# A fused alignment and FFN kernel: dense lead products on TensorE, and clears and mask preparation moved from GpSimd to VectorE ahead of the context's landing

## What is computed

```python
def align_one(small, large):                 # small: context 64x256, large: layernorm(x) 512x256
    D = sqrt(maximum(|small|^2 + |large|^2 - 2 small @ large.T, 0))
    R = dtw_cost(D)        # R[i,j] = D[i,j] + min(R[i-1,j], R[i,j-1], R[i-1,j-1])
    i_idx, j_idx, valid = backtrack(R)       # argmin of diagonal, up, left
    return zeros(512, 256).at[j_idx].add(small[i_idx] * valid)

x = x + vmap(align_one)(ctx, layernorm(x))
x = x + quantised_linear(relu(fixed_quant(quantised_linear(layernorm(x), w1, b1))), w2, b2)
```

## Time and profile before

| | us |
|---|---|
| median of 3 runs | 184.52 |
| the three runs | 184.53, 183.70, 184.52 |
| span of the profiled execution, first to last instruction | 182.2 |
| around the span, against the median | 2.3 |
| DVE busy | 154.0 (85%) |
| PE busy | 110.1 (60%) |
| ACT busy | 105.2 (58%) |
| POOL busy | 40.4 (22%) |

### The profile page before, as it was taken

The page is one execution under the profiler, slowest core; times in us unless marked ns, Lnnn a source line. Parts: engine busy times, 40 slices in busy tenths (PEclk is TensorE's granted clock), DMA queues, the critical chain, the costliest instruction groups (busy, mean ns, idle before and its releaser), DMA issues.

```text
span 182.2 us, 3483 instructions
## 1 busy us (share of the span) xinstructions
PE 110.1 (60%) x1109; PEld 76.7 (42%) x1109; DVE 154.0 (85%) x737; ACT 105.2 (58%) x195; POOL 40.4 (22%) x101
## 2 busy tenths in 40 slices
PE   6999970000267500000004878999999999989990
PEld 6799960000146200000001334655666666656670
DVE  4999968999999999999999179998898989894441
ACT  3777685899992000053150079878777786877710
POOL 7955894000000000000000000014051322223150
PEclk9999997555555885555555899999999999999999
DMA  4995018300079600010203421005463729193666
GB/s 158 351 351 186 5 14 351 127 0 0 2 244 338 230 0 0 0 60 14 72 14 116 70 37 24 4 0 61 58 62 53 77 45 104 18 112 34 81 66 168
DMA packets 19602, 16.88 MB, mean 93 GB/s; under 512 B 5760, under 2 KB 19200, under 8 KB 19456
## 3 DMA queue, kind: packets, MB, share of 16 engines
q1 hardware_dynamic: 14336, 12.69, 21.5%
q0 software_dynamic: 3808, 3.67, 17.1%
q10 hardware_dynamic: 1440, 0.30, 0.8%
HBM read 7.48 MB, written 9.18 MB: 91 GB/s over the span
## 4 chain that ended last, share of the span: by engine, by line
DVE 43%; PE 30%; DMA 8%; POOL 6%; ACT 3%; issue 3%; SPq 2%; ACTq 1%; DVEq 0%; POOLq 0%
PE y L1330 12%; PE h L1311 8%; DMA X<-in_x_dram 6%; DVE Y L1089 6%; DVE R L873 6%; PE t L1311 4%; DVE A L841 3%; DVE enter L1076 3%; DVE carry L861 3%; DVE bcarry L1075 3%; DVE M L862 3%; PE e L1270 3%; POOL lengths L461 3%; SPq L317 2%; DVE Y L1086 2%
## 5 line engine op out<-in xcount | busy, mean ns | idle before, releaser
L482 POOL DMA_DIRECT2D out_dram<-E x14 | 17.0, 1217 | 129.8 <-DVE E L1060 129.8
L1330 PE MATMUL y<-w2T,XT 128*128 128x256 bf16 x256 | 37.7, 273 | 0.4 <-DVE XT L1050 0.4
L1330 PEld LDWEIGHTS y<-w2T,XT 128*128 128x128 bf16 x256 | 24.9, 98 | 14.7 <-DVE XT L1050 0.7
L1348 PE MATMUL h<-w1T 128*128 128x512 bf16 x21 | 6.5, 463 | 36.5 <-DVE XT L969 36.5
L653 ACT ACTIVATE h_int<-h,b_s 128x512 int16<-128x512 f32 x37 | 25.3, 686 | 4.9 <-PE h L1311 4.3
L1311 PE MATMUL h<-M,w1T 128*128 128x512 bf16 x74 | 21.9, 380 | 0.5 <-ACT M L646 0.4
L659 ACT ACTIVATE code<-Y,shifts 128x640 bf16<-128x640 bf16 x3 | 2.5, 829 | 31.5 <-DVE enter L1076 31.5
L1050 DVE TENSOR_SCALAR XT<-h_int 128x1024 bf16<-128x1024 int16 x28 | 12.1, 439 | 8.6 <-ACT h_int L653 8.6
L1254 PE MATMUL t<-ident_bf,w_raw 128*128 128x128 bf16 x32 | 4.6, 312 | 24.3 <-ACT w_raw L587 22.7
L1348 PEld LDWEIGHTS h<-w1T 128*128 128x128 bf16 x21 | 2.2, 116 | 40.4 <-DVE XT L969 37.3
L653 ACT ACTIVATE h_int<-t,b_s 128x512 int16<-128x512 f32 x19 | 13.0, 686 | 3.3 <-PE t L1311 3.0
(11 more groups left out here) (231 smaller groups left out, 291.2 us busy)
## 6 DMA issues: line engine op xcount, KB each, us to landing
X<-in_x_dram SPq DMA_DIRECT2D x8, 512.0 KB, 9.1
out_dram<-b_s SPq DMA_DIRECT2D x7, 512.0 KB, 5.6
out_dram<-E POOLq DMA_DIRECT2D x14, 256.0 KB, 4.3
w_raw<-in_L_ffn_w_dram SPq DMA_DIRECT2D x2, 1024.0 KB, 5.9
S<-in_ctx_dram SPq DMA_DIRECT2D x1, 512.0 KB, 4.0
out_dram<-E SPq DMA_DIRECT2D x4, 128.0 KB, 3.0
path_dram<-A SPq DMA_DIRECT2D x3, 160.0 KB, 1.8
path_dram<-XT SPq DMA_DIRECT2D x3, 160.0 KB, 1.9
```

Source lines behind the costliest of these rows:

```text
L482: nc.gpsimd.dma_start(tiles_out[:, b:b + 2, quad_of(g), :], res[:, g % 2, 2 * h:2 * h + 2, :], accum_op=ALU.add).then_inc(out_stored[g % 2 ...
L1330: mm = nc.tensor.matmul(bank67[t // 2][:, t % 2, :], hq[:, g % 2, n, t * P:t * P + P], w2T[:, n, :], start=(n == 0 and not bias), stop=(n ...
```

## The change

The lead becomes ten products of the whole identity with itself, 128 weight columns by 128 moving columns. The clears of ident and of the six mask tensors, and the two clears of Dm, are done by DVE at the head of its list instead of by POOL; the Dm clears have a semaphore of their own, column_made. All of first_masks stands behind masks(), ahead of the context's statistics. Its wait for the POOL constants becomes a wait for column_made, a wait for mask 12 is added inside it, and DVE waits for the eight remaining constants behind order_masks.

```diff
-LEAD = 40
+LEAD = 10
...
+        column_made = sem("column_made")
...
         def _(pool):
-            nc.gpsimd.memset(ident[:, :], 0.0).then_inc(ident_made, 1)
             pool.wait_ge(ident_made, 1)
             nc.gpsimd.affine_select(out=ident[:, :], in_=ident[:, :], compare_op=ALU.not_equal, fill=1.0, base=0,
                                     pattern=[[-1, P]], channel_multiplier=1).then_inc(ident_made, 1)
-            for i, (t, n) in enumerate(((first_of, P // CH), (upper_of, (CH + 1) * NQ * 2), (lower_of, (CH + 1) * NQ * 2),
-                                        (half_of, NQ * 2 * CH), (batch_of_u, NQ * 2 * CH), (column_batch, 4 * CH))):
-                nc.gpsimd.memset(bass.AP(t, 0, [[n, P], [1, n]]), 0.0).then_inc(masks_made, 1)
             pool.wait_ge(masks_made, 6)
...
-            nc.gpsimd.memset(Dm[:, 0, 0:1], 0.0).then_inc(slot_const, 1)
-            nc.gpsimd.memset(Dm[:, 1:SLOTS, 0:1], 0.0).then_inc(slot_const, 1)
...
             def first_masks():
-                v.wait_ge(slot_const, 10)
+                v.wait_ge(column_made, 2)
                 v.wait_ge(dve_order, own[0])
...
                 nc.vector.tensor_tensor(last_row[:, :], upper[:, 0:CH], lower[:, 1:CH + 1], ALU.add).then_inc(dve_order, 1)
+                v.wait_ge(masks_made, 12)
                 nc.vector.tensor_scalar(other[:, :], column_batch[:, :, :, :].rearrange("p e h c -> p (e h c)"), odd_batch[:, :],
                                         None, ALU.subtract).then_inc(dve_order, 1)
...
+            nc.vector.memset(ident[:, :], 0.0).then_inc(ident_made, 1)
+            for t, n in ((first_of, P // CH), (upper_of, (CH + 1) * NQ * 2), (lower_of, (CH + 1) * NQ * 2),
+                         (half_of, NQ * 2 * CH), (batch_of_u, NQ * 2 * CH), (column_batch, 4 * CH)):
+                nc.vector.memset(bass.AP(t, 0, [[n, P], [1, n]]), 0.0).then_inc(masks_made, 1)
+            nc.vector.memset(Dm[:, 0, 0:1], 0.0).then_inc(column_made, 1)
+            nc.vector.memset(Dm[:, 1:SLOTS, 0:1], 0.0).then_inc(column_made, 1)
             v.wait_ge(ident_made, 2)
...
             masks()
+            first_masks()
 
             v.wait_ge(ctx_loaded, 16)
...
             load_moments(0)
-            for j in range(B // 2):
-                moments(1, j)
-            first_masks()
-            for j in range(B // 2, UL):
-                moments(1, j)
+            load_moments(1)
             load_moments(2)
             scales(0)
...
             order_masks()
+            v.wait_ge(slot_const, 8)
             v.wait_ge(rooted, 2 * LOADS + 2)
...
             for i in range(LEAD):
-                nc.tensor.matmul(bank5[0:TW, 0:8], ident[:, 0:TW], ident[:, 0:8], start=True, stop=True)
+                nc.tensor.matmul(bank5[:, 0:P], ident[:, :], ident[:, :], start=True, stop=True)
```

## The result

The change makes the kernel slower: 185.05 us median of seven runs against 183.93 us for the kernel before, run beside it; the ratio is 1.0053 with a 95% interval of 1.0033 to 1.0072. The profiled span grows from 182.2 to 183.3 us.

A forecast was written before the change was run, and what follows sets the result against it. The bound was taken to be x loads, DVE statistics and POOL up to to_chunks at 32.87 us; earlier X20 and X21, partly lost to X31 and interlock, gain 0.25 us from 184.5: forecast 184.3 us, range 183.3 to 185.2.

The forecast's parts named there:

- The bound: Loads of x, DVE statistics, POOL, then DVE; the whole effect is how much earlier to_chunks starts, now at 32.87 us.
- Part 4: first_masks early on DVE: 1.52 us long, what follows at most 0.65 us late against 1.4 us of room; worth 0.
- Part 3: Clears on DVE: 0.15 us of them show; POOL's masks and everything behind come 0.45 us earlier; worth 0.
- Part 5: Fewer PE instructions move the code packet to 13.1 us plus up to 1; X20, X21 on time, X30, X31 late.
- Rival B: Code block behind the last load's packets, 16.1 us or later: all loads land on time, 183.3 us; chance 0.19.
- Parts 1 and 2: PE's lead ends between 4.2 and 6.5 us, clock lifts by 5 to 9, dots(0) near 12.4; worth 0 on the path.
- C: More POOL operations caught inside DVE ones from 16.8 to 29.6 us, three at 0.42 to 0.45 each: 185.5 us; chance 0.16.
- nothing behind 33 us: Nothing is edited after to_chunks; any change behind 33 us larger than the one at 33 would make the argument wrong.

The follow-up runs named there:

- lead_short: The kernel before with ten of the tiny lead products in place of forty; 183.03 us, ratio 0.9968 to the kernel before.
- clears_alone: The kernel before with only the clears moved from POOL to DVE; 184.10 us, ratio 1.0008 to the kernel before.
- clear_twice: The changed kernel with POOL's clear of E done twice in a row; 186.97 us, ratio 1.0171 to the kernel before.
- one_input_early: The changed kernel with only four one-input mask operations ahead of the context, the rest in the middle of load 1; 185.82 us in one run.
- lead_tiny: The changed kernel with the old lead of forty tiny products; 185.35 us, ratio 1.0076 to the kernel before.
- clear_waits: The changed kernel with POOL making its small constants first, then waiting for first_masks before clearing E; 182.87 us, ratio 0.9947 to the kernel before.
- pool_waits: The changed kernel with one added wait: POOL, behind its iotas, waits for first_masks before its small constants and clear of E; 182.66 us, ratio 0.9934.
- lead_alone: The kernel before with only the new dense lead; 183.05 us, ratio 0.9965 to the kernel before.
- masks_mid: The changed kernel with first_masks back between the halves of load 1; 183.55 us, ratio 0.9982 to the kernel before.

## Why the prediction was wrong

**The bound, and its effect at 33 us: right for the change as a whole.** It acts through the start of to_chunks: +1.34 us there, +1.1 in the span, +0.98 by the ratio. For the lead by itself it isn't: lead_short gains more behind 33 us than at 33, which the prediction named as a sign that its argument is wrong (below).

**Part 4, the step that failed.** "1.52 us behind the last mask reduction" priced first_masks by a row from 10.93 us, where POOL reads and writes tiny tensors or waits. At its new place POOL is in an unbroken run of constants. In the kernel before that run was in plain sight, though I put neither row into the working; POOL's timeline there, 4 to 7 us:

```profile
4.12 0.17 POOL L407 MEMSET M<- 128x40 f32 x1
...
4.79 2.26 POOL L416 MEMSET E<- 128x2600 f32 x1
```

The measured price at the new place is 4.2 us (3.46 to 7.66), 1.5 of work and 2.7 of being held. "At most 0.65 us late against 1.4 us of room: 0" was 2.9 us late, so the room was spent more than twice.

**Part 3:** POOL's list did come forward, the clear of E from 4.79 to 4.12, and so did the end of the mask reductions, from 3.91 to 3.34. Whether this made the hold longer or shorter isn't shown, since no run has the masks early and the clears on POOL. The clears themselves are free (clears_alone).

**Part 5, the code packet: right in kind, wrong in time.** X20 and X21 landed at 12.5 and 14.1, but the packet came at 16.9, not between 13 and 15. I counted to the packet's start in the kernel before (212 records, 209 by the trace) as if the count set it. In the nine kernels with a lead of ten products it starts at 16.05 to 16.25, about 1 us before the last load lands, in six (322 to 347 records gone), and at 16.9 to 20.0, with 236 to 252 records gone, in the three whose PE came that far only then (the changed kernel, clear_twice, one_input_early). With a lead of forty it starts at 10.2 to 10.5, with 192 to 209 records gone. So a request probably waits behind queued loads; that was not tried by itself. Rival B's premise (all loads on time) was nearly met, with X30 at 16.1 in place of 16.7 and X31 at 17.5 in place of 18.1; B's 183.3 us did not follow, since the landings no longer set the pace.

**Parts 1 and 2:** the lead ended at 6.2 (4.2 to 6.5 forecast) and the clock rose in the range given, but dots(0) started at 16.05, not 12.4, because ctx_len and the centring came 3.1 us late. PE stayed off the chain, as said.

**The rivals.** C named a slower outcome by the interlock of POOL and DVE, at 185.5, which is 1.0 us above the kernel before, as measured. That is luck: its place (POOL's spread and lengths behind 16.8 us), its form (two-input operations) and its price (0.43 us each) were all other than what happened: POOL's stretch from 20 us on is the same seven held operations, shifted whole. It was the right resource and the wrong side; DVE waited for POOL, not POOL for DVE.

**What "nothing behind 33 us" missed.** lead_short gains 0.2 us at to_chunks but 0.6 by its ratio and 1.0 in its span. Behind to_chunks, PE's later code packets move as well: in the kernel before the ninth one starts at 176.30 us, among the last stores, and lead_short has eight. From the start of the last DVE result to the end of the span it is 3.8, 4.0 and 3.5 us in the three profiles with a packet there (before, clears_alone, lead_tiny) and 3.1 to 3.6 in the nine without. Between to_chunks and that last result it is 145.3 to 145.9 us in all twelve profiles. The later tail would cover most of the rest, but the two ranges overlap, one profile stands for each kernel and it wasn't tried by itself, so it stays open.

## What to carry to other kernels

Price a moved operation by what its new neighbours do on the engine that shares its way to SBUF, not by its duration at the old place: ask of VectorE's TENSOR_SCALAR operations whether GpSimd is doing anything at that time, and of its two-input ones whether GpSimd is reading; statistics of one input went through untouched here. If GpSimd has time, a wait on GpSimd is the cheap cure; here one line turned +0.5% into -0.7%. And count the instructions of an engine before a stage of heavy loads: a block of code is a transfer too, and with fewer instructions it came after the loads instead of among them.

## What was not expected of the hardware

- A VectorE operation that is held shows no wait in the trace: its record starts on time and only its end is late (3.12 us for 39 elements, and 2.96 us for one element behind it).
- A run of short GpSimd memsets, 0.10 to 0.32 us each and overlapping, held VectorE like one long one: 1.62 us in clear_waits, 0.26 us in pool_waits for the same operation. A later run of the same kind, 6.46 to 7.80 in the changed kernel, cost each operation at most 0.1 us.
- Four BATCH_NORM_STATS2 take 1.41 us whether GpSimd clears 128x2600 beside them (pool_waits, from 4.96) or subtracts two tensors (the changed kernel, from 7.69).
- With a 16 KB code packet at 10.51 us (kernel before) three loads land 1.5 us and a fourth 0.8 us later than in lead_alone, where it starts at 16.08. An 8 KB one at 12.0 to 14.3 us goes with one gap of 2.1 us between loads in place of 1.5, in three of the four kernels that have one there.
- Ten dense products lift the granted clock to 1.00 (2.4 GHz) by 7.8 us in place of 12.6; PE then had 2.05 us without work, and it stood at 0.50 (1.2 GHz) from 11.2 to 14.4 us. In lead_alone and masks_mid, with the same lead and no such wait, it was 1.00 in both stretches.
